# Whole chunks in the last tile, normalisation in halves, and later splits of output units in a cross-attention kernel

## The reference

```python
enc = encoder_hidden_states[:, :end_pos, :]     # 2044 of 2048 rows
ca = encoder_hidden_states[:, end_pos:, :]      # the last 4, the tokens
query, keyt, valt = hidden_states @ Wq, enc @ Wk, enc @ Wv
hs = _mha(query, keyt, valt)                    # 8 heads, softmax
ca_q1 = jnp.einsum('btc,th->bch', ca, Wq_ca)[:, indices, :]
ca_hs1 = _mha(ca_q1, residual, residual)
ca_hs2 = _mha(ca_hs1 @ Wq, ca @ Wk_ca, ca @ Wv_ca)
out = (hs + ca_hs2) @ Wout + b_out + residual
```

## Time and profile before

| | |
|---|---|
| median of 3 runs | 1199.17 us |
| the profiled execution | 1199.81 us, of which the span is 1197.8 us |
| granted clock of TensorE | 1.00 |
| TensorE matmul busy | 99% |
| VectorE busy | 69% |
| ScalarE busy | 57% |
| POOL busy | 18% |

### The profile page before, as it was taken

One profiled execution on the slowest core, in us unless ns is written; L12 is line 12 of the kernel. 1 busy time (PEld: TensorE's weight loads), 2 busy tenths in 40 slices (PEclk: granted clock), 3 DMA queues, 4 the chain that ended last, 5 costly groups with the idle time before them and its releaser, 6 DMA issues.

```text
span 1197.8 us, 14824 instructions
## 1 busy us (share of the span) xinstructions
PE 1189.5 (99%) x5649; PEld 965.1 (81%) x5649; DVE 826.5 (69%) x1181; ACT 680.4 (57%) x797; POOL 210.7 (18%) x123
## 2 busy tenths in 40 slices
PE   9999999999999999999999999999999999999999
PEld 7888888788666677888888888888888888888998
DVE  7468625771144388888888888888888888886551
ACT  5323433222644467777677777777777777778210
POOL 1100000011000021222222222222221221221233
PEclk9999999999999999999999999999999999999999
DMA  8975785693920084354454455445436436422254
GB/s 310 352 271 177 266 299 212 224 322 113 293 50 1 1 199 99 97 125 111 111 120 112 106 116 127 101 105 137 106 90 152 100 80 155 134 68 67 91 196 154
DMA packets 139376, 178.08 MB, mean 149 GB/s; under 512 B 79705, under 2 KB 97113, under 8 KB 135466
## 3 DMA queue, kind: packets, MB, share of 16 engines
q1 hardware_dynamic: 131690, 156.36, 46.1%
q0 software_dynamic: 2864, 10.24, 2.6%
q10 hardware_dynamic: 4752, 10.55, 2.6%
HBM read 113.72 MB, written 63.24 MB: 148 GB/s over the span
## 4 chain that ended last, share of the span: by engine, by line
PE 95%; DVE 2%; DMA 1%; issue 1%; ACT 1%; SPq 0%; DVEq 0%; ACTq 0%
PE at_ps L1330 28%; PE bank L726 20%; PE at_ps L1311 19%; PE at_ps L243 9%; PE acc_t_ps L1091 7%; PE at_ps L1520 6%; PE s_ps L1059 2%; PE bank L703 1%; DVE prob_lo L1186 1%; DMA x_f<-in_xT 1%; PE acc_t_ps L1070 1%; PE f_ps L243 1%; PE f_ps L1012 1%; PE f_ps L1022 0%; PE at_ps L1523 0%
## 5 line engine op out<-in xcount | busy, mean ns | idle before, releaser
L259 DVE TENSOR_REDUCE mpart<-at_ps 128x1 f32<-128x512 f32 x480 | 324.6, 685 | 90.8 <-PE at_ps L243 89.2
L1249 ACT ACTIVATE prob_hi<-at_ps 128x1024 fp32r<-128x1024 f32 (+1 forms) x256 | 263.3, 1028 | 178.9 <-PE at_ps L1311 176.8
L1330 PE MATMUL at_ps<-prob_hi,v 128*128 128x512 f32 (+1 forms) x1024 | 315.0, 393 | 0.0
L1186 DVE TENSOR_TENSOR prob_lo<-probs,prob_hi 128x1024 fp32r<-128x1024 f32 (+1 forms) x211 | 273.5, 1296 | 21.3 <-ACT probs L1254 20.7
L1254 ACT ACTIVATE probs<-at_ps 128x1024 f32<-128x1024 f32 (+1 forms) x256 | 261.6, 1022 | 0.0
L1330 PEld LDWEIGHTS at_ps<-prob_hi,v 128*128 128x128 f32 (+1 forms) x1024 | 191.1, 188 | 43.7 <-ACT x_hi_place L1263 1.7
L1186 POOL TENSOR_TENSOR prob_lo<-probs,prob_hi 128x1024 fp32r<-128x1024 f32 x45 | 108.0, 2400 | 501.6 <-ACT probs L1254 501.6
L243 PE MATMUL at_ps<-a 128*128 128x512 f32 x480 | 189.0, 394 | 0.4 <-DVE mpart L259 0.4
L1330 PE MATMUL at_ps<-prob_lo,v 128*128 128x512 f32 (+1 forms) x512 | 158.7, 391 | 0.5 <-DVE prob_lo L1186 0.5
L1311 PE MATMUL at_ps<-a 128*128 128x512 f32 (+1 forms) x512 | 158.7, 391 | 0.2 <-DVE vw L965 0.2
L1311 PE MATMUL at_ps<-b 128*128 128x512 f32 (+1 forms) x512 | 158.1, 390 | 0.0
(11 more groups left out here) (160 smaller groups left out, 1392.8 us busy)
## 6 DMA issues: line engine op xcount, KB each, us to landing
v_hi_d<-v_t SPq DMA_DIRECT2D x16, 648.0 KB, 6.3
v_lo_d<-v_t SPq DMA_DIRECT2D x16, 648.0 KB, 8.1
v<-v_hi_d SPq DMA_DIRECT2D x16, 648.0 KB, 5.5
v<-v_lo_d SPq DMA_DIRECT2D x16, 648.0 KB, 7.2
k_hi_d<-out_hi SPq DMA_DIRECT2D x40, 256.0 KB, 4.9
k_lo_d<-out_lo SPq DMA_DIRECT2D x40, 256.0 KB, 5.9
a<-k_hi_d SPq DMA_DIRECT2D x16, 640.0 KB, 7.6
b<-k_hi_d SPq DMA_DIRECT2D x16, 640.0 KB, 11.2
```

The source lines that it names most:

```text
L259: dve.tensor_reduce(self.mpart[:, g % 2, qt, c:c + 1], at[:, 0:w], AX, ALU.max).then_inc(self.mx_done, 1)
L1186: eng.tensor_tensor(pl[n % PL][0:r, :], prob[n % PF][0:r, :], ph[n % PB][0:r, :].bitcast(F32), ALU.subtract).then_inc(sem, 1)
L1249: act.activation(ph[n % PB][0:r, :], s_ps[n % 2][0:r, :], ACT.Exp, scale=SCALE).then_inc(ph_done, 1)
L1330: mm = pe.matmul(wide[3][:, u], a[0:r, t, :], y[0:r, u * CH:(u + 1) * CH], start=t == 0 and m == 0, stop=t == KT - 1 and m == 2)
```

## The change

The maxima's products take 512 columns in every chunk, the scores of tile 15 take 128 columns of weights and its values 128 rows. What the four extra rows of `v` give must be nothing: a fourth memset sets rows 96 to 127 of tile 15 to zero, and the loads of v write only 124 rows of tile 15, so each becomes two DMAs. VectorE and ScalarE keep their 508 columns and 124 rows. POOL normalises in two halves, in steps 10 and 11, each after the low part of the tile n + 1. In head 15 the last three blocks of the output units are split after the last low part.

```diff
+FILLS = 4
...
     def fill_ones(self, pool, p):
...
+        pool.wait_ge(self.kb_ones, FILLS * p + 3)
+        pool.memset(self.v_s[p][3 * 32:P, :, KT - 1, 0:DA].bitcast(F32), 0.0).then_inc(self.kb_ones, 1)
...
     def load_v(self, sp, scratch, g):
         for i, src in enumerate((scratch["vh"], scratch["vl"])):
-            sp.dma_start(self.v_s[g % 2][:, i, :, 0:DA].bitcast(F32), src[g].rearrange("p (t d) -> p t d", d=DA)
-                         ).then_inc(self.v_in[g % 2], 16)
+            of = src[g].rearrange("p (t d) -> p t d", d=DA)
+            for rows, tiles in ((slice(0, LASTK), slice(0, KT)), (slice(LASTK, P), slice(0, KT - 1))):
+                sp.dma_start(self.v_s[g % 2][rows, i, tiles, 0:DA].bitcast(F32), of[rows, tiles]
+                             ).then_inc(self.v_in[g % 2], 16)
...
     def score_piece(self, pe, mx_ps, g, k):
...
-            w = min(CH, SK - c * CH)
-            pe.matmul(to[:, 0:w], self.queries_a(g)[:, qt * P:(qt + 1) * P], self.keys_a(g)[:, c * CH:c * CH + w],
+            pe.matmul(to, self.queries_a(g)[:, qt * P:(qt + 1) * P], self.keys_a(g)[:, c * CH:(c + 1) * CH],
...
-    def normalise(self, pool, g):
+    def normalise(self, pool, g, u):
         p = g % 2
+        half = slice(u * CH, (u + 1) * CH)
         pool.wait_ge(self.rbc_in, (g + 1) * 16)
-        pool.tensor_tensor(self.o_raw[p][0:D, :], self.o_raw[p][0:D, :], self.rbc[:], ALU.mult
+        pool.tensor_tensor(self.o_raw[p][0:D, half], self.o_raw[p][0:D, half], self.rbc[:, half], ALU.mult
                            ).then_inc(self.norm_done, 1)
-        pool.wait_ge(self.norm_done, g + 1)
+        pool.wait_ge(self.norm_done, 2 * g + u + 1)
...
         def gpsimd(pool):
...
-                if t == 11 and g:
-                    at.normalise(pool, g - 1)
+                if t in (10, 11) and g:
+                    wait_low(pool, n + 1)
+                    at.normalise(pool, g - 1, t - 10)
...
         def vector(dve, early_split):
...
-                if g == G - 1:
+                if g == G - 1 and t < KT - 3:
                     early_split(dve, t)
+            for t in range(KT - 3, KT):
+                early_split(dve, t)
...
             def scores(n, between):
...
-                        mm = pe.matmul(s_ps[n % 2][0:r, u * CH:(u + 1) * CH], a[:, t * P:t * P + r],
+                        mm = pe.matmul(s_ps[n % 2][:, u * CH:(u + 1) * CH], a[:, t * P:(t + 1) * P],
...
             def values(n, between):
...
-                        mm = pe.matmul(wide[3][:, u], a[0:r, t, :], y[0:r, u * CH:(u + 1) * CH],
+                        mm = pe.matmul(wide[3][:, u], a[:, t, :], y[:, u * CH:(u + 1) * CH],
```

More of the change, by code:

```diff
@@ L186, in fill_ones @@
         pool.memset(self.keys_b(p)[3 * 32:P, :].bitcast(F32), 1.0).then_inc(self.kb_ones, 1)
-        pool.wait_ge(self.kb_ones, 3 * p + 1)
+        pool.wait_ge(self.kb_ones, FILLS * p + 1)
         pool.memset(self.queries_b(p)[3 * 32:P, :].bitcast(F32), 0.0).then_inc(self.kb_ones, 1)
-        pool.wait_ge(self.kb_ones, 3 * p + 2)
+        pool.wait_ge(self.kb_ones, FILLS * p + 2)
         pool.memset(self.v_s[p][:, :, :, DA:P].bitcast(F32), 0.0).then_inc(self.kb_ones, 1)
+        pool.wait_ge(self.kb_ones, FILLS * p + 3)
+        pool.memset(self.v_s[p][3 * 32:P, :, KT - 1, 0:DA].bitcast(F32), 0.0).then_inc(self.kb_ones, 1)
     def load_a(self, sp, scratch, g):
@@ L234, in score_piece @@
         n = g * STEPS + k
-        to = mx_ps[n % 2]
+        to = mx_ps[n % 2][:]
         if k == 0:
@@ L288, in spread @@
         if g:
-            eng.wait_ge(self.norm_done, g)
+            eng.wait_ge(self.norm_done, 2 * g)
         eng.dma_start(self.rbc[:, None, :], scratch["rden"][None, g:g + 1, :].to_broadcast([D, 1, SQ])
                       ).then_inc(self.rbc_in, 16)
-    def normalise(self, pool, g):
+    def normalise(self, pool, g, u):
         p = g % 2
+        half = slice(u * CH, (u + 1) * CH)
         pool.wait_ge(self.rbc_in, (g + 1) * 16)
-        pool.tensor_tensor(self.o_raw[p][0:D, :], self.o_raw[p][0:D, :], self.rbc[:], ALU.mult
+        pool.tensor_tensor(self.o_raw[p][0:D, half], self.o_raw[p][0:D, half], self.rbc[:, half], ALU.mult
                            ).then_inc(self.norm_done, 1)
-        pool.wait_ge(self.norm_done, g + 1)
+        pool.wait_ge(self.norm_done, 2 * g + u + 1)
     def put(self, eng, scratch, g):
         p = g % 2
-        eng.wait_ge(self.norm_done, g + 1)
+        eng.wait_ge(self.norm_done, 2 * (g + 1))
         eng.dma_start(scratch["hs"][g * D:(g + 1) * D, :], self.o_raw[p][0:D, :]).then_inc(self.hs_out[p], 16)
@@ L845, in sync @@
             sp.dma_start(onehot_f, d["onehot"]).then_inc(oh_in, 16)
-            sp.wait_ge(at.kb_ones, 3)
+            sp.wait_ge(at.kb_ones, FILLS)
             at.load_b(sp, scratch, 0)
@@ L859, in gpsimd @@
             at.fill_ones(pool, 0)
-            pool.wait_ge(at.kb_ones, 3)
+            pool.wait_ge(at.kb_ones, FILLS)
             pool.memset(at.one[:], 1.0).then_inc(at.one_done, 1)
@@ L1190, in sync @@
             gathered(sp, B)
-            sp.wait_ge(at.kb_ones, 6)
+            sp.wait_ge(at.kb_ones, 2 * FILLS)
             at.load_b(sp, scratch, 1)
@@ L1229, in gpsimd @@
             at.fill_ones(pool, 1)
-            pool.wait_ge(at.kb_ones, 6)
+            pool.wait_ge(at.kb_ones, 2 * FILLS)
             for n in range(N):
@@ L1301, in scores @@
                 g, t = divmod(n, KT)
-                r = keys(n)
                 if t == 0:
@@ L1318, in values @@
                 g, t = divmod(n, KT)
-                r = keys(n)
                 if t == 0:
-                    pe.wait_ge(at.v_in[g % 2], (g // 2 + 1) * 32)
+                    pe.wait_ge(at.v_in[g % 2], (g // 2 + 1) * 64)
                 pe.wait_ge(ph_done, n + 1)
@@ L1334, in values @@
                 mm.then_inc(pv_done, 1)
-            pe.wait_ge(at.kb_ones, 3)
+            pe.wait_ge(at.kb_ones, FILLS)
             gathered(pe, 1)
@@ L1455, in gpsimd @@
                 add_bias(n)
-            at.normalise(pool, G - 1)
+            for u in range(2):
+                at.normalise(pool, G - 1, u)
             for n in range(2, NT_OUT):
```

## The result

| | before | after |
|---|---|---|
| median | 1199.26 us (1199.14 to 1199.42, 4 runs) | 1221.7 us (1217.21 to 1223.31, 4 runs) |
| ratio after / before | | 1.0181 [1.0157, 1.0205] |
| the profiled execution | 1199.81 us, span 1197.8 us | 1217.21 us, span 1215.4 us |

The change makes the kernel slower by 22.4 us, or 1.8%. The runs of before lie within 0.3 us, those of after within 6, and the profiled one is the fastest of the four: its rows explain 17.6 us of span, and 4.5 us of the median lie in executions without a trace.

A forecast was written before the change was run, and what follows sets the result against it. TensorE, busy 99% of the span, bounds the kernel, so only its waits count. Terms +2.3 + 7.5 + 1.5 - 0.5 + 0 = +10.8 us on 1199.81, less 0.64 to the median: 1210.0 us, range 1205 to 1214 (1196.5 to 1214 with rivals).

The forecast's parts named there:

- token stage: Copies of the token maxima, queued behind v's narrow load, land late and stall TensorE once: +7.5 us, bounds 5.6 and 9.6.
- head 1: Head 1's shift row, queued behind v and Wout, comes late for TensorE: +1.5 us, at most 2.3.
- Later loads of v cost nothing more: In the heads after head 1, v's narrow loads land with enough lead: 0 us.
- heads' halves: POOL's two halves in 14 heads: 2.3 us gained at step 10, 4.6 lost at the negation, net +2.3 us.
- whole chunks: Padding to 128 rows gains 0.7 us, maxima products of 512 columns cost 0.2: together -0.5 us.
- last head: Later split of output units gains 0.8 us, halves delaying low parts cancel it: 0, bounds -0.8 and +1.0.
- The four engines: v's 124-row loads run on four DMA engines of sixteen: 19.1 us instead of 4.8, everything queued behind 14.3 us later.
- I take the wait: VectorE's negation of the maxima waits for POOL's second half: TensorE stalls 0.33 us in 14 heads, +4.6 us.
- B: Rival: loads of v stay wide or have lead enough, the negation waits for POOL; 1201.0 us, chance 0.14.
- C: Rival: wide loads, nothing waits for POOL at the second half; 1195.6 us, chance 0.15, of which 0.12 faster.
- A: Rival: narrow loads of v, but the negation does not wait for POOL; 1206.6 us, chance 0.20.
- signs of the right case: v's second issue some 16 us, landing some 20; share near 0.3; idle 6-10 us near 343; low part 1.22; negation's load idle 0.3.

The follow-up runs named there:

- e2: The kernel before with only the loads of v split into 124 rows with 16 tiles and 4 rows with 15: 1222.96 us, ratio 1.0208.
- e3: The kernel before with only the normalisation in halves behind low parts: 1202.49 us, ratio 1.0025.
- e5: The kernel before with only the whole chunks, and v loaded wide (128 rows for 15 tiles, 112 and 12 for tile 15): 1197.96 us, ratio 0.9988.
- e1: The changed kernel with v loaded wide (128 rows for 15 tiles, 112 and 12 rows for tile 15): 1199.66 us, ratio 1.0003.
- e9: e8 with v loaded as 120 rows with all tiles, 8 rows with 15 tiles and 4 rows of tile 15: 1193.67 us, ratio 0.9953.
- e7: e1 with the halves of the normalisation one step earlier, in steps 9 and 10: 1194.56 us, ratio 0.9959.
- e8: e7, but in the last head POOL's halves do not wait for low parts: 1193.78 us, ratio 0.9956.
- e6: The changed kernel, narrow loads kept, with head 0's load of v issued behind the token maxima's copies: 1215.79 us, ratio 1.0132.

## Why the prediction was wrong

The sign, the likeliest case and its mechanisms held; the time, 1221.7 us, lies 11.7 us above the 1210.0 of the forecast and 7.7 above the range's end. Three steps failed: the fall of the clock was left out of sum and range, head 1's stall was bounded too low, and the later loads of v were put at nothing. Of the 11.7 us, 6.6 lie in the profiled execution; the other 5.1 are by how much the medians differ from the profiled runs, and no trace shows them. The terms one by one, forecast against the profiled run and the experiments:

| term | forecast | measured |
|---|---|---|
| token stage | +7.5 (5.6 to 9.6) | +11.1: 8.8 idle, 2.3 clock |
| head 1 | +1.5 (0 to 2.3) | +5.5: 4.1 idle, 1.4 clock |
| "Later loads of v cost nothing more" | 0 | about +1.1 in after, +4.8 in e2 |
| heads' halves | +2.3 | +2.1 in e3 |
| whole chunks | -0.5 | -1.5 in e5 |
| last head | 0 | 0 |

**The clock.** "The granted clock is 1.00 in all rows; should it fall after the token stage's idle stretch, that comes on top and no row prices it." It fell, after both stretches, and cost 2.3 and 1.4 us. The step that failed is leaving it out of sum and range: together 3.7 us, more than the 3.2 by which the profiled execution (1217.21) lies above 1214. Rows of before couldn't size it, for they don't show how long the clock stays down; but at half the clock each matmul costs its 0.227 us once more, and an allowance of some matmuls behind each stretch of idle belonged in the upper end.

**The four engines.** "By the same count 124 rows go to **four** engines" held: share and rate fell to a quarter, e1 and e2 show that the loads' shape is the cause, and e9 that it isn't the missing multiple of 16. 19.1 us was near: 67 GB/s for four is 16.8 each instead of 17.4, and a pair's packets took 21.7 us in the steady head, against 5.4 in before. The bounds of the token wait held 8.8; its middle, 7.5, counted on engines that were early, and was 1.3 us short.

**Head 1.** "Wout is issued at 440.48 and lands 8.9 later, at 449.4, then 463.7" failed by its size. Against TensorE, itself 11.0 us late from the tokens, Wout landed not 14.3 us later but 476.04 - 449.38 - 11.0 = 15.7: SyncE held it back by 16.5 us, and it then landed in 8.0 instead of 8.9. TensorE needed the shift row at 476.51 - 4.18 = 472.3, and it came behind Wout: 3.7 us, and some 0.5 more for the row itself. So the bound of 2.3 was too low by 1.9 us. The 1.5 also counted on engines that were early, and the run shows no such gain.

**SyncE and the later loads.** "SyncE itself is held in the issue, some 16 us instead of 2, and is free before the store" held in the steady head, but barely: both parts together held it 20 us instead of 2.6, and it was free 1.3 us before the store, where the forecast had left some 5. In the head of e2 shown above it was held 23 us and released at the moment of store and shift row, and TensorE waited 1.67 us for the row. "Later loads of v cost nothing more" failed for that reason: heads 2 to 14 lost 4.8 us in e2 and 1.3 in after; with wide loads (e1) they lost 0.1 to 0.2, so about 1.1 of after's 1.3 are the loads'. That this also explains the scatter, and the part of the miss that no trace shows, is argued and not shown.

**The negation.** "I take the wait" held: 0.60 us, in e3 as in after. TensorE's loss at it was 0.22 us rather than 0.33, and 0.2 more at the copy of its row behind, which the sum had not. In e3 the 14 heads gain 3.0 us at step 10 and lose 5.2 behind the negation, where the forecast had 2.3 and 4.6: both sizes were low, and the net came out near by luck. e7 removes the wait; there the halves give 0.24 us a head against e5, where the forecast had 0.17.
The Trainium skill (SBUF — State Buffer, Who interferes with whom) holds that tensor_scalar and copies can take ports that GpSimd can hold for a whole instruction, and that on this chip a reduce never does; the runs agree (0.60 against 0.17 us for eight columns, 1.51 against 0.42 for a copy, 0.19 for the reduce in front).

**Whole chunks.** "Ten matmuls a head at 3 to 6 ns" was near in size, but only the six of the values have it (5.8 ns), 0.6 us in 16 heads; the four of the scores have nothing. What failed is "4 of 512 columns of 0.227 us is 1.8 ns, 128 times: +0.2 us": the wider product costs 0.8 ns more itself, but the three behind it come 14 ns sooner. With 128 of them that is some -1.7 us instead of +0.2. The interval of e5 (-2.5 to -0.4) reaches down to the forecast all the same.

**Rivals.** B, wide loads, is e1: 1199.66 us instead of 1201.0, the chunks' 1.0 and some 0.3 making the difference. C, wide loads where nothing waits for POOL's second half, is nearest to e7: 1194.56 instead of 1195.6. Its number came near by other terms than its own, for the halves and chunks gave more than C had, and the last head's 0.8 was not gained there (e8 gains it). A is excluded by 0.60 us of the negation. The range's lower end, 1196.5, is called C's, though C's own sum is 1195.6.

**What showed it.** Four signs of the right case appeared: the share of 0.32, a single idle stretch near 343 of 8.8 us, the low part of tile 10 at 1.22 in every head, and the idle ahead of the load of the negation (0.45 us, not 0.3). The one on SyncE's issue appeared in another form: v's second part took 9.6 us and not 16, and both parts 20. The narrow loads have no landing in the trace, so that sign can't be read as it was put; the packets of the pair end 23 us after its first issue (717.45 to 740.7).

The Trainium skill (DMA: Bandwidth & Descriptors, Why a DMA increments its semaphore by 16 and not by 1) lets a DMA use the largest divisor up to 16 of its slowest dimension; the runs agree for 124 rows (a share of 0.32 against 1.27), and for 120 they exclude a narrow load (1.29) but can't tell 15 engines from 16.

## What to carry to other kernels

Before trimming a DMA to the rows that matter, look at what its row count divides by: 124 rows instead of 128 cost 22 us here, and a few more DMAs of wide shapes cost nothing. Leave room in the forecast for TensorE's clock wherever it predicts idle of microseconds. Follow a slow transfer on its issuing queue and not only by its landing: what is queued behind is issued late, and the last transfer with a deadline decides. When shared work is moved off one VectorE instruction, look which instruction takes its place: one step earlier was worth 0.36 us a head.

## What was unexpected in the hardware

- TensorE's granted clock was 0.50 (1.2 GHz) for about 4 us after 8.8 us of idle, and for about 3 us after 4.1 us of idle; it cost 2.3 and 1.4 us. In e6, after 6.1 us of idle, it was 0.50 for some 6 us.
- SyncE is held about 10 us in issuing one part of v on four engines, where it was about 2 us or less on sixteen; behind a full queue the pair took 28 to 32 us, where it was 12 to 15.
- A one-input operation on eight columns, 0.17 us alone, waits to the end of POOL's instruction (0.60 us). A copy of 512 columns went from 0.42 to 1.51 us.
- A maxima product of 508 columns instead of 512 saved 1 ns itself, and the three matmuls behind it started 14 ns later in all.
- Loads of 120 rows moved 156 GB/s where those of 128 rows moved 277, at the same DMA share.
